# Adding the results of expert tiles straight into the output, with a wait for the last landing only at a change of expert

## The reference, cut to what matters

```python
logits = jnp.einsum('btc,ec->bte', x, router_w)          # 16 experts
top_vals, top_idx = jax.lax.top_k(logits, 2)             # 2 of them per token
gates = jax.nn.sigmoid(top_vals)
w_full = jnp.zeros((N, E)).at[jnp.arange(N)[:, None], sel].add(gw)
gu = jnp.einsum('nc,ech->neh', xf, gate_up_w)            # 256 -> 2 * 256
gate, up = jnp.split(gu, 2, axis=-1)
h = jax.nn.silu(gate) * up
out_all = jnp.einsum('neh,ehc->nec', h, down_w)          # 256 -> 256
moe = jnp.einsum('ne,nec->nc', w_full, out_all)
return moe + shared            # shared: one dense expert for all tokens; x is added outside
```

## Time and profile before

| what | us |
|---|---|
| median of three executions | 1447.92 (1446.27 to 1452.80) |
| profiled execution, own time | 1457.63 |
| its span | 1455.8 |
| PE busy in the span | 1280.3 (88%) |
| DVE busy | 904.8 (62%) |
| ACT busy | 669.9 (46%) |
| GpSimd (POOL) busy | 498.1 (34%) |
| stretch from the last shared product to the span's end (1279 to 1455.8) | 176.8 |

### The profile page before, as it was taken

How to read it: one execution, slowest core, us unless ns; L and a number is a source line. 1 busy time by engine, 2 the same in 40 slices (tenths; PEclk the granted TensorE clock), 3 DMA queues, 4 the chain that set the end, 5 groups by cost and what they waited for, 6 DMA issues and landing times. The chain is left out here.

```text
span 1455.8 us, 18087 instructions
## 1 busy us (share of the span) xinstructions
PE 1280.3 (88%) x5674; PEld 574.7 (39%) x5674; DVE 904.8 (62%) x2078; ACT 669.9 (46%) x1245; POOL 498.1 (34%) x734
## 2 busy tenths in 40 slices
PE   4798989989998999998988988986889889999991
PEld 2232422423343234543543543542242335566661
DVE  4799878788886775475475475477567423233334
ACT  2255455565545555465455455454546550122220
POOL 5434241163222212344244244235222212236651
PEclk9699999999999999999999999998999789999996
DMA  7742412425312233222222222225422005612225
GB/s 245 225 131 80 139 58 75 124 58 175 119 49 66 59 88 102 67 76 63 66 75 64 66 72 67 66 78 94 114 81 45 16 15 162 216 45 79 82 57 173
DMA packets 113007, 135.84 MB, mean 93 GB/s; under 512 B 15745, under 2 KB 92037, under 8 KB 112659
## 3 DMA queue, kind: packets, MB, share of 16 engines
q1 hardware_dynamic: 105075, 122.01, 28.9%
q0 software_dynamic: 5664, 10.57, 2.5%
q10 hardware_dynamic: 2176, 2.10, 0.4%
HBM read 87.57 MB, written 48.53 MB: 93 GB/s over the span
## 5 line engine op out<-in xcount | busy, mean ns | idle before, releaser
L1252 DVE TENSOR_REDUCE Mx<-bank 128x1 f32<-128x512 f32 x512 | 341.3, 686 | 256.0 <-PE bank L994 254.2
L890 ACT ACTIVATE prob<-bank 128x512 f32<-128x512 f32 x576 | 334.2, 596 | 304.3 <-PE bank L1020 303.3
L994 PE MATMUL bank<-KS,QS 96*128 96x512 bf16 x768 | 300.7, 392 | 40.4 <-DVE Mx L1252 16.7
L1020 PE MATMUL bank<-QS,KS 99*128 99x512 bf16 x768 | 300.1, 392 | 40.0 <-DMA QS<-MR 14.5
L1033 PE MATMUL bank<-prob,V 128*17 128x512 f32 x1536 | 210.1, 620 | 0.7 <-ACT prob L890 0.7
L890 ACT ACTIVATE prob<-prob 128x512 f32<-128x512 f32 x192 | 120.9, 630 | 154.2 <-DVE prob L1263 153.3
L1020 PEld LDWEIGHTS bank<-QS,KS 99*128 99x128 bf16 x768 | 75.3, 99 | 239.6 <-ACT prob L890 113.6
L994 PEld LDWEIGHTS bank<-KS,QS 96*128 96x128 bf16 x768 | 75.9, 99 | 186.6 <-DVE Mx L1249 53.3
L735 POOL TENSOR_SCALAR MR<-neg 16x128 bf16<-16x128 f32 x48 | 13.8, 288 | 267.5 <-ACT neg L865 267.2
L1249 DVE CUSTOM_DVE_ANT_0 bank<-bank,ff_h 128x512 f32<-128x512 f32 x128 | 88.0, 695 | 24.2 <-PE bank L994 23.8
L1249 DVE CUSTOM_DVE_ANT_0 bank<-bank,mask 128x512 f32<-128x512 f32 x128 | 87.6, 698 | 21.2 <-PE bank L994 20.8
(11 more groups left out here) (176 smaller groups left out, 1849.3 us busy)
## 6 DMA issues: line engine op xcount, KB each, us to landing
stack_scr<-parts SPq DMA_DIRECT2D x48, 384.0 KB, 2.6
QS<-stack_scr SPq DMA_DIRECT2D x48, 384.0 KB, 4.1
KS<-stack_scr SPq DMA_DIRECT2D x48, 384.0 KB, 5.1
stack_scr<-parts SPq DMA_DIRECT2D x48, 256.0 KB, 2.9
w_gu<-in_gate_up SPq DMA_DIRECT2D x16, 512.0 KB, 9.7
stack_scr<-parts SPq DMA_DIRECT2D x48, 128.0 KB, 2.8
cT<-in_ctxT SPq DMA_DIRECT2D x8, 512.0 KB, 5.7
w_dn<-in_down SPq DMA_DIRECT2D x16, 256.0 KB, 9.9
```

The source lines that it names most:

```text
L890: act.activation(prob[:, u % NP_, j, :], src, ACT.Exp, scale=CAST).then_inc(exp_done, 1)
L994: pe.matmul(bankS[i % NS][:, :], QS[0:STACK, h, qt * P:(qt + 1) * P], KS[0:STACK, h, :], start=True, stop=True).then_inc(s_full, 1)
L1020: pe.matmul(bankT[e % NT][:, :], KS[0:ROWS, h, kt * P:(kt + 1) * P], QS[0:ROWS, h, :], start=not on_pe, stop=True).then_inc(t_full, 1)
L1252: dve.tensor_reduce(dst, b, AX.X, ALU.max).then_inc(s_read, 1)
```

## The change

1. **Destination.** `y_tok` is gone. A scatter now adds its rows to `out` in DRAM (`compute_op=ALU.add`). For that, SP stores `acc` (residual and shared expert) to `out` first, in four stores of 512 KB behind the weight loads, and GpSimd waits for all four before its first scatter. The token table holds the same number for both choices of a token, so `home` is the token itself.
2. **Order of the scatters.** Two tiles of one expert never hold the same token, two tiles of different experts may. Every scatter waits on a semaphore `apart`, which SP raises. For s = 1 and 2 SP first waits for the landing of scatter s - 1. From s = 3 it reads a number from the table `landings`: where tile s has another expert than tile s - 1 it stands for the landing of scatter s - 1, otherwise for that of scatter s - 3. DVE makes that table with three more small instructions in `tile_experts`.
3. **Rows ahead.** `NX` is 32 instead of 8, on 8 semaphores (a gather waits for the one 8 before it); the other 16 gathers follow every second scatter.
4. **Start of the loop.** PE transposes the rows of tiles 0 and 1 ahead of the last `down_products`, DVE copies them ahead of the last `add_shared`, and PE's wait for `y_read` stands in iteration 1, behind two gate/up products.
5. **Addresses.** `token` is one instruction on `tag` instead of four.
6. **Tail.** The loads of `got`, the 32 adds and the 8 stores are gone. SP waits for the last two scatters, and the program ends.

```diff
-                pool.iota(tags[:, :, :, 0], [[P, TT], [SLOTS, 2]], base=0, channel_multiplier=1,
+                pool.iota(tags[:, :, :, 0], [[P, TT], [0, 2]], base=0, channel_multiplier=1,
...
-        NX = 8
-        NR = 4
+        NX = 32
+        ROWS_SEM = 8
...
             def _(sp):
...
-                for i in range(2):
-                    sp.wait_ge(yt_out[i], 16 * (TILES // 2))
-                o = out.rearrange("b (t p) n -> (b t) p n", p=P)
...
-                for t in range(0, TT, 2):
-                    if t >= NR:
-                        sp.wait_ge(added, t - NR + 1)
-                    sp.dma_start(got[:, t % NR, :, :], y[t]).then_inc(got_in[t % NR], 16)
-                    if t >= NR:
-                        store(t - NR)
...
+                o = out.rearrange("b (t p) n -> b p t n", p=P)
+                for b in range(B):
+                    if b >= EARLY_SHARED:
+                        sp.wait_ge(y_read, (b - EARLY_SHARED + 1) * QT)
+                    sp.dma_start(o[b], acc[:, b * QT:(b + 1) * QT, :]).then_inc(rows_out, 16)
+                sp.wait_ge(landings_ready, 1)
+                for s in range(1, TILES):
+                    last = sum_out[(s - 1) % 2]
+                    if s <= 2:
+                        sp.wait_ge(last, 16)
+                    else:
+                        sp.wait_ge(last, sp.value_load(landings[0:1, s:s + 1], min_val=16, max_val=8 * TILES))
+                    sp.sem_inc(apart, 1)
                 for i in range(2):
+                    sp.wait_ge(sum_out[i], 16 * (TILES // 2))
...
+                pool.iota(landed[0:1, 1:TILES + 1], [[16, TILES // 2], [0, 2]], base=0, channel_multiplier=0,
+                          allow_small_or_imprecise_dtypes=True).then_inc(consts, 1)
...
                 def rows(s):
+                    if s >= ROWS_SEM:
+                        pool.wait_ge(xr_in[s % ROWS_SEM], 16 * (s // ROWS_SEM))
                     if s >= NX:
                         pool.wait_ge(xT_full, s - NX + 1)
...
                 for s in range(NX):
                     rows(s)
+                pool.wait_ge(rows_out, 16 * B)
                 for s in range(TILES):
+                    if s:
+                        pool.wait_ge(apart, s)
                     pool.wait_ge(yt_read, s + 1)
-                    if s >= 2:
-                        pool.wait_ge(yt_out[s % 2], 16 * (s // 2))
-                    pool.indirect_dma_start(y_tok, bass.IndirectOffsetOnAxis(home[:, s:s + 1], 0),
-                                            yt[:, s % 2, :], None, bounds_check=2 * SLOTS - 1,
-                                            oob_is_err=False).then_inc(yt_out[s % 2], 16)
-                    if s + NX < TILES:
-                        rows(s + NX)
+                    pool.indirect_dma_start(sums, bass.IndirectOffsetOnAxis(home[:, s:s + 1], 0),
+                                            yt[:, s % 2, :], None, bounds_check=SLOTS - 1, oob_is_err=False,
+                                            compute_op=ALU.add).then_inc(sum_out[s % 2], 16)
+                    if s % 2 == 0 and NX + s // 2 < TILES:
+                        rows(NX + s // 2)
...
-                down_products(LATE - 1)
...
+                pe.wait_ge(hid_done, LATE * HT - 1)
                 turn_rows(0)
                 turn_rows(1)
+                down_products(LATE - 1)
                 pe.wait_ge(w_in, 32 * NE)
-                pe.wait_ge(y_read, LATE * QT)
...
+                    if s == 1:
+                        pe.wait_ge(y_read, LATE * QT)
...
+                    link(dve.tensor_tensor(first_of[:, 1:TILES], texp[:, 1:TILES], texp[:, 0:TILES - 1], ALU.not_equal))
+                    link(dve.scalar_tensor_tensor(out=first_of[:, 1:TILES], in0=first_of[:, 1:TILES], scalar=16.0,
+                                                  in1=landed[:, 1:TILES], op0=ALU.mult, op1=ALU.add))
+                    dve.tensor_copy(landings[:, 1:TILES], first_of[:, 1:TILES]).then_inc(landings_ready, 1)
...
-                    link(dve.tensor_scalar(second[:, :], tag[:, :], float(SLOTS), -float(SLOTS), ALU.is_ge, ALU.mult))
-                    link(dve.tensor_tensor(second[:, :], tag[:, :], second[:, :], ALU.add))
-                    link(dve.tensor_scalar(second[:, :], second[:, :], SLOTS - 1.0, None, ALU.min))
-                    dve.tensor_copy(token[:, :], second[:, :]).then_inc(token_ready, 1)
+                    dve.tensor_scalar(token[:, :], tag[:, :], SLOTS - 1.0, None, ALU.min).then_inc(token_ready, 1)
...
-                for t in range(TT):
-                    dve.wait_ge(got_in[t % NR], 16 * (t // NR + 1))
-                    for k, s in enumerate((first, added)):
-                        dve.tensor_tensor(acc[:, t, :], got[:, t % NR, k, :], acc[:, t, :], ALU.add).then_inc(s, 1)
-                        if k == 0:
-                            dve.wait_ge(first, t + 1)
```

More of the change, by code:

```diff
@@ L1425, in experts @@
         tile_expert = sb("tile_expert", [1, TILES], I32)
-        got = sb("got", [P, NR, 2, D], F32)
         hid = sb("hid2", [P, 2, HT, S], F32)
@@ L1442, in experts @@
         gate = sb("gate", [P, TILES], F32)
-        second = sb("second", [P, TILES], F32)
+        first_of = sb("first_of", [1, TILES], F32)
+        landed = sb("landed", [1, TILES + 2], F32)
+        landings = sb("landings", [1, TILES], I32)
         home = sb("home", [P, TILES], U32)
@@ L1465, in experts @@
         chain2 = sem("chain2")
-        xr_in = [sem(f"xr_in{i}") for i in range(NX)]
+        xr_in = [sem(f"xr_in{i}") for i in range(ROWS_SEM)]
         xT_full = sem("xT_full")
@@ L1475, in experts @@
         yt_read = sem("yt_read")
-        yt_out = [sem(f"yt_out{i}") for i in range(2)]
-        got_in = [sem(f"got_in{i}") for i in range(NR)]
-        first = sem("first")
-        added = sem("added")
-        stored = sem("stored")
+        sum_out = [sem(f"sum_out{i}") for i in range(2)]
+        rows_out = sem("rows_out")
+        landings_ready = sem("landings_ready")
+        apart = sem("apart")
         tokens_of = t_scr.rearrange("b s n -> (b s) n")
         table_of = tag_scr.rearrange("(r q) c -> r (q c)", q=P)
-        y = y_tok.rearrange("(k t p) n -> t p k n", p=P, k=2)
+        sums = out.rearrange("b s n -> (b s) n")
         with nc.Block() as block:
```

27 lines of the change are left out of this document (8 added, 19 removed).

## The result

The changed kernel took 1436.63 us (median of 13 executions, 1432.35 to 1442.77), the kernel before, beside it, 1449.30 us (13 executions, 1446.25 to 1454.33). The ratio is 0.992, with a 95% interval of 0.990 to 0.993: 12.7 us faster, half of the 26.1 us that were forecast. The profiled execution took 1437.58 us, its span is 1435.8 us.

What follows compares the result with a forecast made beforehand. PE bounds the loop, with a read-back tail behind: -24.6 (tail) - 1.74 (loop start) + 0.2 (table) + 0.0 (scatters) = -26.1 us, from median 1447.92 to 1421.8, rounded up to 1422.5; likeliest 1419 to 1425 (0.57), range up to 1444.

Steps and rivals of the forecast that it cites:

- The bound and its place: The tile loop is PE's alone, 3.02 us per iteration; PE stands still at its start, and a 24.50 us stretch follows.
- The start: Start of the loop: transposes fill PE's 1.41 us gap, so the first gate/up product starts 1.74 us sooner.
- the cover of the gathers: Ahead of the loop: 32 gathers take 40 us, to 1284.7, leaving GpSimd 3.0 us ahead of the first scatter.
- the table term: Start of the loop: one more small GpSimd constant makes the table arrive perhaps 0.2 us later, which PE would show.
- The scatters: the term in doubt: Adding scatters in the tile loop: landing after 3.2 us, instruction 1.02 us, no loss to PE, 0.0 in the sum.
- L: Time from an adding scatter's start to its landing: taken as 3.2 us, bounded by 2.4 and 5.3.
- the 47 waits: Stepping through the loop's scatter waits: no loss up to a 3.6 us landing, 4 us at 3.8, 37 at 5.3.
- The sum of parts: Adding scatter's landing: 2.1 us fixed, 0.8 for reading rows as a gather, 0.3 for writing them, together 3.2 us.
- "The number of row pairs is the same": Reason given for GpSimd's adding-scatter instruction staying at 1.02 us, with 2.0 us as the upper bound.
- "All of the 24.6 us between goes": Tail: everything from the last scatter's landing at 1431.17 to the span's end at 1455.8 disappears, -24.6 us.
- The last landing: End of the loop: the nine empty tiles' scatters move nothing and stay at 2.1 us to landing.
- Case (a): Rival in the loop: longer landings or GpSimd instruction make PE wait 2 to 20 us; 1424 to 1442 us, chance 0.23.

Runs made afterwards that it cites:

- e14: Changed kernel with plain instead of adding scatters and a GpSimd memset behind each: loop 139.7 us, part 248.6 us, which holds a 26 us stall.
- e15: Changed kernel with plain scatters and four more SP register loads between landing and signal: loop 171.0 us, part 284.8 us, which holds a 26 us stall.
- e2: Changed kernel with all its waits of order, but plain scatters that overwrite instead of adding: ratio 0.986 to the kernel before, loop 139.8 us.
- e3: Changed kernel with scatters adding into scratch rows of their own, without waits of order: ratio 0.984 to the kernel before, loop 139.7 us.
- e12: Changed kernel without the scatters of the last six tiles, which are empty: ratio 0.984 to the kernel before, part 218.7 us.

## What was right in the prediction, and the steps that failed

- **The bound and its place: right.** PE's loop, its start and the read-back tail were the three places. That the loop was PE's alone is what the earlier trace rows shows, with PE busy for 142.00 of 142.00 us at a granted clock of 1.00. The start gave 1.74 us to the hundredth, the cover of the gathers held (the last of the 32 ended at 1277.7, the first scatter started at 1281.04, behind ACT), and the table term of 0.2 us can't be seen. The first three stores of `acc` took up to 13.8 us to land, where the earlier trace rows had 5.0 at most; that cost nothing, as the fourth, which counts, took 3.4 us and had landed at 1276.4.
- **The step that failed in the loop: "The scatters: the term in doubt".** It took L = 3.2 us, and measured was 3.7; it took GpSimd's instruction at 1.02 us, and measured was 1.56. Its term of 0.0 in the sum measured +7.5 us. The mechanism was the one described (a pair of tiles, the buffers, Silu behind the scaling), and both ends of the range held the values (2.4 to 5.3, 1.02 to 2.0). PE's waits began sooner than said, in the iteration of tile 10 and not from tile 15 on. Going through the 47 waits again by hand with the measured 1.56 and 3.7 gives an estimate of +7.5 us, which is what the loop lost; with 1.02 and 3.7 it gives +1.6, with 1.56 and 3.2 nothing. That each length alone would be cheap is argued by this estimate and not shown, since e14 and e15 did not set them apart. That the addition needs the order to cost the loop anything is shown by e2 and e3.
- **Why 3.2 was too little.** The sum of parts let the read and the write share one fixed part of 2.1 us. But even an addition with no row in it lands after 2.7 us, which is 0.6 us more, about as much as GpSimd's instruction is longer (0.54). The rows were priced well: 0.8 + 0.3 = 1.1 us reckoned, 3.7 - 2.7 = 1.0 measured. It was the fixed part that failed. "The number of row pairs is the same" was no reason for an equal instruction: the trace had never shown one that adds. That the added read costs no more than a gather's rows was the prediction's estimate; no run sets the read and the write apart. The 3.7 us were measured in a loop that moves 45 GB/s at a DMA share of 0.34 (68 GB/s and 0.23 before).
- **The step that failed at the end: "All of the 24.6 us between goes".** 4.8 us stayed, GpSimd's drain. It could have been read off the trace of before: the DRAIN row from 1428.9 to 1438.7 ends 7.6 us behind the last landing (1431.17), and with the tail gone it is what ends last. The tail had covered it, and the prediction did not name it. It now ends 7.4 us after the last scatter's start instead of 9.7, which no row of before told.
- **The last landing, left at nothing.** The last scatter starts 8.5 us after the last gate/up in both kernels, but with no row in it an addition lands later than the "2.1" us of the prediction. Up to the moment at which SP sees it that costs 0.8 us.
- **The rivals.** Case (a), landings or a longer instruction eat a part of the gain, "1424 to 1442 us", is what came, with both of its causes. It had 0.23 against 0.57. What spoke for it was that two lengths were unknown and the gain was at its full only with both near their lower end; no row of an addition favoured the lower end, and so (a) deserved the larger chance.

## What to carry to other kernels

An operation that the trace has never shown should be priced with its issuing instruction and its landing both unknown, and where a chain of waits is steep in either (here 22 us per us, by the prediction's estimate), the forecast belongs to the middle of the range, not to its flat end. In a chain with order, count what one element can make up after a wait (3.02 - 1.86 us here) beside what the wait costs. Before a tail is struck out, look at what the engines' sequencers do under it: work that ended with indirect GpSimd transfers kept GpSimd's sequencer 4.8 us beyond the last landing here (7.5 us with plain scatters), and that goes under other work if the last transfer comes early (in e12 the drain was over 5.4 us ahead of the span's end).

## What the runs showed of the hardware

- A scatter of 128 rows of 1 KB that adds takes GpSimd 1.56 us and lands after 3.7 us; a plain one takes 0.99 to 1.02 and 2.4 us. Without rows: 2.7 against 2.1 us.
- The DRAIN of GpSimd at the block's end is over 6.9 to 7.6 us after the start of the last adding scatter, and 9.6 to 9.8 us after that of the last plain one.
- Four register loads on SP between a wait and a signal put 2.1 us between the two (e15), and with them SP released only one scatter in 3.0 us.
- On two of the five chips of the experiments, a burst of 32 gathers went with 26 us more in the shared expert, most of which ACT and DVE spent waiting. The cause is open.
